# Cross-attention and mixture-of-experts block on one core: every product as plain 32-bit matmuls in two column halves, in place of three products of split operands

## The reference, cut to what matters

```
x = x + xattn(layernorm(x), ctx, w_q, w_k, w_v, w_o, b_o)
x = x + ffn(layernorm(x), router_w, router_b, w1, b1, w2, b2)
```

## Time and profile before

| | |
|---|---|
| median of three runs | 1013.3 us (1012.0 to 1015.47) |
| the profiled execution | 1018.17 us, its span 1016.3 us |
| TensorE busy | 979.9 us, 96% of the span |
| VectorE, ScalarE, GpSimd busy | 769.2, 624.3, 284.2 us |
| granted TensorE clock, mean | 0.993 |

### The profile page before, as it was taken

One profiled execution on the slowest core, in us unless ns is written; L12 is line 12 of the kernel. 1 busy time (PEld: TensorE's weight loads), 2 busy tenths in 40 slices (PEclk: granted clock), 3 DMA queues, 4 the chain that ended last, 5 costly groups with the idle time before them and its releaser, 6 DMA issues.

```text
span 1016.3 us, 23196 instructions
## 1 busy us (share of the span) xinstructions
PE 979.9 (96%) x8382; PEld 883.9 (87%) x8382; DVE 769.2 (76%) x2088; ACT 624.3 (61%) x1736; POOL 284.2 (28%) x440
## 2 busy tenths in 40 slices
PE   7889999999999999999999999999888999999996
PEld 6778888888888888888888888888678999999996
DVE  6897768878787888878787887878755666776662
ACT  5777767777776777777676777777514333344330
POOL 5542021314223131313223131311442333222233
PEclk9999999999999999999999999999999999999998
DMA  8440101101010101101010110001105543444522
GB/s 241 144 114 2 33 2 33 43 13 55 14 40 15 33 13 33 44 2 43 12 32 6 33 35 6 17 5 50 58 18 178 137 96 80 113 128 129 136 26 26
DMA packets 48431, 56.74 MB, mean 56 GB/s; under 512 B 5324, under 2 KB 44218, under 8 KB 48192
## 3 DMA queue, kind: packets, MB, share of 16 engines
q1 hardware_dynamic: 39488, 46.30, 14.7%
q0 software_dynamic: 8832, 8.98, 5.5%
HBM read 36.01 MB, written 24.20 MB: 59 GB/s over the span
## 4 chain that ended last, share of the span: by engine, by line
PE 71%; DVE 18%; ACT 5%; issue 4%; DMA 0%; POOLq 0%; POOL 0%; another core or an unknown queue 0%; ACTq 0%
PE psum L561 29%; PE psum L756 11%; PE psum L658 8%; PE psum L644 7%; PE psum L628 7%; PE psum L672 7%; DVE prob L985 5%; ACT prob L819 3%; DVE negmax L974 3%; DVE kl L922 1%; DVE al L922 1%; PE psum L566 1%; DVE stats L929 1%; PE psum L719 1%; DVE ql L963 1%
## 5 line engine op out<-in xcount | busy, mean ns | idle before, releaser
L819 ACT ACTIVATE prob<-psum,negmax 128x256 f32<-128x256 f32 x512 | 239.1, 484 | 81.6 <-DVE negmax L974 81.6
L771 ACT ACTIVATE probt<-psum 128x512 f32<-128x512 f32 x256 | 157.6, 617 | 53.4 <-PE psum L644 51.1
L974 DVE TENSOR_REDUCE negmax<-psum 128x2 f32<-128x512 f32 x256 | 160.0, 683 | 22.0 <-PE psum L628 21.9
L985 DVE TENSOR_SCALAR prob<-prob,invtot 128x256 f32<-128x256 f32 x512 | 168.0, 392 | 4.5
L644 PE MATMUL psum<-ident,prob 128*128 128x128 f32 x1024 | 154.4, 275 | 3.3 <-DVE prob L985 1.7
L644 PEld LDWEIGHTS psum<-ident,prob 128*128 128x128 f32 x1024 | 120.5, 142 | 14.5 <-issue 4.4
L898 ACT ACTIVATE hid<-psum,b1t 128x640 f32<-128x640 f32 x64 | 50.9, 795 | 133.2 <-PE psum L561 133.2
L658 PE MATMUL psum<-probt,v 128*64 128x256 f32 x1024 | 124.6, 385 | 0.8 <-ACT probt L771 0.8
L541 POOL DMA_INDIRECT out_rows<-y,rowi x40 | 65.7, 1644 | 174.5 <-DVE y L1137 169.6
L505 POOL DMA_INDIRECT slot_table<-row,picki x64 | 64.7, 1011 | 170.2 <-DVE picki L1087 143.2
L819 ACT ACTIVATION_READ_ACCUMULATOR prob<-psum,negmax 128x1 f32 x512 | 111.2, 217 | 0.0
(11 more groups left out here) (159 smaller groups left out, 2738.4 us busy)
## 6 DMA issues: line engine op xcount, KB each, us to landing
w1r<-in_w SPq DMA_DIRECT2D x8, 1024.0 KB, 8.1
w2r<-in_w SPq DMA_DIRECT2D x8, 1024.0 KB, 10.4
slot_table<-blank SPq DMA_DIRECT2D x8, 662.5 KB, 9.8
rows<-slot_table SPq DMA_DIRECT2D x7, 662.5 KB, 5.4
xin<-in_x SPq DMA_DIRECT2D x16, 256.0 KB, 3.0
out_rows<-x SPq DMA_DIRECT2D x16, 256.0 KB, 3.2
c<-in_ctxt SPq DMA_DIRECT2D x16, 128.0 KB, 3.1
c<-in_ctxt SPq DMA_DIRECT2D x32, 64.0 KB, 2.9
```

The costliest lines, as they stand in the source:

```text
L771: copy = lambda dst, src, **kw: act.activation(dst, src, ACT.Copy, **kw)
L819: last = act.activation(prob[:, m % 2, u, qb, :], psum[:, u, qb * S:(qb + 1) * S], ACT.Exp, bias=negmax[:, m % 2, u, qb:qb + 1], accum_out ...
L974: dve.tensor_reduce(negmax[:, m % 2, u, :], psum[:, u, :].rearrange("p (q s) -> p q s", q=ST), AX.X, ALU.max, negate=True).then_inc(sem("m ...
L985: last = dve.tensor_scalar(prob[:, m % 2, u, qb, :], prob[:, m % 2, u, qb, :], invtot[:, m % 2, u, qb:qb + 1], None, ALU.mult)
```

## The change

All splits go. Every operand is kept once in plain 32 bits, and every product is issued in two halves of 64 stationary columns, whose outputs lie in the two halves of the PSUM partitions. `scores` are issued as four 64-row by 64-column tiles for each query block. Turnings become products with the unit matrix, also in two halves. `warm` issues plain 32-bit products over the whole width. Weights are loaded once and stay in place; w1 and w2 of an expert go straight to one of two buffers, the first two during the attention. The 64 unused rows of `wk_s`, `c1` and `wv_s` are zeroed once by VectorE. The copies from PSUM that are left: ScalarE does `xt`, `q`, `v`, the turned probabilities and `x2t`; VectorE does `k`, `pv` and the turned rows. GpSimd loses the context split and the weight splits. The rows ring has three buffers (`RRING`), the context ring three (`CRING`). `hid` keeps all 8 blocks of an expert. `k(0)` is moved ahead of `xt(0)`.

```diff
-    xt, q, k = "xt xt_hi xt_lo", "q q_hi q_lo", "k k_hi k_lo"
-    pv = "pv a_hi a_lo"
+    xt, q, k, pv = "xt xt_sb", "q q_sb", "k k_sb", "pv a_sb"
+    out = [*steps("ln1_stats ln1_root ln1", 0), ("warm", 28), *steps(k, 0), ("warm", 8), *steps(xt, 0),
+           *steps(q, 0), *steps("scores max0 max1 exp0", 0), *steps(q, 1), *steps("max2 max3", 0), *steps(k, 1),
...
             def products(dst, terms):
+
                 for j, (lhs, rhs) in enumerate(terms):
-                    mm = pe.matmul(dst, lhs, rhs, start=(j == 0), stop=(j == len(terms) - 1))
+                    for h in range(2):
+                        hs = slice(h * HD, (h + 1) * HD)
+                        mm = pe.matmul(dst[hs, :], lhs[:, hs], rhs, start=(j == 0), stop=(j == len(terms) - 1))
                 return mm
+
+            def turned(dst, src):
+                return products(dst, [(src, ident[:, :])])
 
             def warm(at):
                 for j in range(at):
-                    pe.transpose(psum[:, 4, j % 4 * P:(j % 4 + 1) * P], ident[:, :], ident[:, :])
+                    pe.matmul(psum[:, 4, j % 4 * P:(j % 4 + 1) * P], ident[:, :], ident[:, :], start=True, stop=True)
...
                     mm = products(dst[:, cc * S:(cc + 1) * S],
-                                  [(w[:, k, cols], a[:, b % 2, k, :]) for k in range(DC)
-                                   for w, a in ((wqh, xth), (wqh, xtl), (wql, xth))])
+                                  [(wq_s[:, k, cols], xts[:, b % 2, k, :]) for k in range(DC)])
...
-                products(dst, [(c0h[:, b % 2, tt], wvh[:, 0, cols]), (c0l[:, b % 2, tt], wvh[:, 0, cols]),
-                               (c0h[:, b % 2, tt], wvl[:, 0, cols]), (c1s[:, b % 2, tt], wvh[:, 1, cols]),
-                               (c1s[:, b % 2, tt], wvl[:, 1, cols])]).then_inc(sem("v"), 1)
+                products(dst, [(c0[:, b % CRING, tt], wv_s[:, 0, cols]),
+                               (c1[:, b % CRING, tt], wv_s[:, 1, cols])]).then_inc(sem("v"), 1)
...
                     for qb in range(ST):
-                        cols = slice(qb * P, (qb + 1) * P)
-                        for j, (a, w) in enumerate(terms):
+                        for half in range(2):
                             for h in range(2):
-                                r = slice(h * HD, (h + 1) * HD)
-                                mm = pe.matmul(psum[:, 2 * cc + h, qb * S:(qb + 1) * S], a[r, m % 2, cc, cols],
-                                               w[r, m % 2, cc, :], start=(j == 0), stop=(j == len(terms) - 1))
+                                r, part = slice(h * HD, (h + 1) * HD), slice(half * HD, (half + 1) * HD)
+                                cols = slice(qb * P + half * HD, qb * P + (half + 1) * HD)
+                                mm = pe.matmul(psum[part, 2 * cc + h, qb * S:(qb + 1) * S], qs[r, m % 2, cc, cols],
+                                               ks[r, m % 2, cc, :], start=True, stop=True)
...
-                        mm = pe.transpose(psum[:, TURN_BANK[u], kb * S + qb * P:kb * S + (qb + 1) * P],
-                                          prob[:, m % 2, u, qb, kb * P:(kb + 1) * P], ident[:, :])
+                        mm = turned(psum[:, TURN_BANK[u], kb * S + qb * P:kb * S + (qb + 1) * P],
+                                    prob[:, m % 2, u, qb, kb * P:(kb + 1) * P])
...
-                    for j, (a, w) in enumerate(((ah, woh), (ah, wol), (al, woh))):
-                        mm = pe.matmul(dst[:, 0:D], a[:, b % 2, c, tt], w[:, c, :], start=(c == 0 and j == 0),
-                                       stop=(c == PAIRS - 1 and j == 2))
+                    for h in range(2):
+                        hs = slice(h * HD, (h + 1) * HD)
+                        mm = pe.matmul(dst[hs, 0:D], a[:, b % 2, c, tt][:, hs], wo_s[:, c, :], start=(c == 0),
+                                       stop=(c == PAIRS - 1))
...
                         mm = products(psum[:, 2 * (at % 2) + half, 0:HALF],
-                                      [(w[:, kk, cols], a[:, r, kk, hs]) for kk in range(DC)
-                                       for w, a in ((w1h[r], bufh), (w1h[r], bufl), (w1l[r], bufh))])
+                                      [(w1_s[:, r, kk, cols], buf[:, r, kk, hs]) for kk in range(DC)])
...
                         if s == 0:
-                            pe.wait_ge(sem("hid_lo"), HC * e + j + 1)
-                        for m, (a, w) in enumerate(((hidh, w2h[r]), (hidh, w2l[r]), (hidl, w2h[r]))):
-                            mm = pe.matmul(dst, a[:, j, ss], w[:, j, :], start=(j == 0 and m == 0),
-                                           stop=(j == HC - 1 and m == 2))
+                            pe.wait_ge(sem("gelu"), HC * e + j + 1)
+                        for h in range(2):
+                            hs = slice(h * HD, (h + 1) * HD)
+                            mm = pe.matmul(dst[hs, :], hid[:, j, s * P + h * HD:s * P + (h + 1) * HD],
+                                           w2_s[:, r, j, :], start=(j == 0), stop=(j == HC - 1))
...
+                if b in (4, 6):
+                    load_w((b - 4) // 2)
...
             def k(n):
-                dve.wait_ge(sem("k_hi"), n + 1)
-                rest_of(kl[:, n % 2, :, :], work_bank("k", n).rearrange("p (c s) -> p c s", c=2),
-                        kh[:, n % 2, :, :]).then_inc(sem("k_lo"), 1)
+                dve.wait_ge(sem("k"), n + 1)
+                if n >= 2:
+                    dve.wait_ge(sem("scores"), 4 * (n - 1))
+                dve.tensor_copy(ks[:, n % 2, :, :], work_bank("k", n).rearrange("p (c s) -> p c s", c=2))\
+                   .then_inc(sem("k_sb"), 1)
```

More of the change, by code:

```diff
@@ L138, in timeline @@
-            *steps("ln2_stats ln2_root", e), ("scatter", c), *steps("x2t x2t_sb logits", d), ("warm", 14),
+            *steps("turn0 copy0", m), *steps("turn1 copy1", m), *steps(half[1], m), *steps("pick scatter", c),
+            ("o", ST * d + 1), ("x2add", ST * d + 1), *steps("ln2_stats ln2_root", d), *steps(pv, m - 1),
+            *steps("turn2 copy2", m), *steps("turn3 copy3", m), *steps(pv, m), *steps("o x2add", ST * e),
+            *steps("o x2add", ST * e + 1), ("ln2", d), *steps("ln2_stats ln2_root", e),
@@ L139, in timeline @@
+            *steps("x2t x2t_sb logits", d), ("warm", 14),
             *steps("bias shift gate_exp gate", d), ("ln2", e), ("rank", d), *steps("x2t x2t_sb", e),
             *steps("pos slot keys", d), ("logits", e), ("warm", 18), *steps("bias shift gate_exp", e),
-            *steps("pick scatter", d), *steps("gate rank pos slot keys pick scatter", e),
-            ("w_lo", 2), ("w_lo", 3), ("warm", 90)]
+            *steps("pick scatter", d), *steps("gate rank pos slot keys pick scatter", e), ("warm", 90)]
@@ new lines, in build @@
+        c1 = sb(es, "c1", [CRING, S])
+        v = sb(es, "v", [2, ST, INNER])
+        a = sb(es, "a", [2, PAIRS, S])
+        x2 = sb(es, "x2", [2, ST, D])
+        row = sb(es, "row", [3, ST, ROW])
+        x2t = sb(es, "x2t", [DC, S])
+        bo_all = sb(es, "bo_all", [D])
+        rwt = sb(es, "rwt", [DC, NE])
+        rb_all = sb(es, "rb_all", [NE])
+        upto = sb(es, "upto", [P], BF16)
+        ones = sb(es, "ones", [P], BF16)
+        lower = sb(es, "lower", [NE, NE])
+        slot0i = sb(es, "slot0i", [NE], I32)
@@ L204, in build @@
+        chosen = sb(es, "chosen", [ST, NE], BF16)
+        before = sb(es, "before", [NE], BF16)
+        pick, same = (sb(es, n, [2, ST]) for n in ("pick", "same"))
+        picki = sb(es, "picki", [3, 2, ST], I32)
         early = ExitStack()
[L205 to L208, removed]
+        prob = sb(early, "prob", [2, UNITS, ST, S])
+        qs = sb(early, "qs", [2, 2, S])
@@ L209, in build @@
+        probt = sb(early, "probt", [2, UNITS, ST, S])
+        ks = sb(early, "ks", [2, 2, S])
         early.close()
[L210 to L218, removed]
@@ L237, in build @@
[L237 to L251, removed]
@@ L264, in build @@
[L264 to L272, removed]
-        def pieces(at):
-            return piece(*SPLITS[at], raw[at])
@@ L940, in ln_apply @@
                 last.then_inc(sem(which), 1)
-            def split(w):
-                dve.wait_ge(sem("split_hi"), w + 1)
-                whole, head, rest_ = pieces(w)
-                rest_of(rest_, whole, head).then_inc(sem("split_lo"), 1)
             def ln1_stats(b):
```

469 lines of the change are left out of this document (156 added, 313 removed).

## The result

The changed kernel takes 1298.85 us (median of four runs, 1298.51 to 1299.15) against 1014.33 us of the kernel before in the same comparison: a ratio of 1.2809, 95% interval 1.2782 to 1.2835. It is slower by 28%. The forecast was 1315 us with a range of 1285 to 1430.

The account below looks back on a forecast made before the run. TensorE, busy 96% of the span, was taken as the bound: 1016.3 + 238 (attention) + 57 (experts) + 10 (warm-up) - 3 (start and rise) = 1318 us of span, forecast about 1315 us, range 1285 to 1430.

Parts of the forecast that it names:

- The main step: In TensorE's products, 128 by 128 with 256 columns takes two pairs of 0.216 us: 0.432 us against 0.36 before.
- Turnings: Each 128 by 128 turning on TensorE goes from 0.11 to 0.216 us; the probabilities' 64 add 6.8 us a batch.
- the rivals: A turning's pairs held by loads (0.27 us each, 1385 us total, chance 0.11) or halves not overlapping (0.432, 1580 us, 0.04).
- factor of four: Skill's rule for turnings: losing the transpose mode makes each 0.44 us, some 1580 us in all; chance 0.04.
- Scores: Sixteen 64 by 64 tiles a period in the attention, four overlapping: 1.93 us against 1.62, +1.2 us a batch.
- rival 1: The four tiles of scores overlap only in twos: +1.73 us a period, +111 us, 1425 us in all; chance 0.12.
- unchanged, 0: The attention's pv already has the new form, so its cost in a batch changes by 0 us.
- The changes of tiling that fall away: Hand-overs saved because most steps now have one tiling: up to -15 or -20 us, within the likeliest case's range.
- `logits` and `pos` keep their form: In the attention's batch sum, these two steps were taken as unaltered and given no added cost.
- start, rise and warm-up together: Opening of the kernel and change-over to the experts: start and rise -3 us, the 90 warm-up products +10.
- The warm-up: The 90 products before the experts hold up the first rows' turning by 90 x 0.11 = 10 us.
- VectorE's and ScalarE's relief: Dropped copies and splits bring 0 in steady state, 5 us either side; TensorE's 6.7 us standstill in the rise counts against start costs.

Follow-up runs that it names:

- Run 7: The kernel before, with a fourth term (remainder by remainder) added to every split product: 1215.16 us against 1019.15, ratio 1.1919.
- run 2: The changed kernel, with products and turnings issued over the whole 128 columns (pv and scores keep their tiles): 1320.77 us, ratio 1.3034.
- run 8: The kernel before, with its 1232 turnings as plain products with the unit matrix over the whole width: 1159.99 us against 1019.15, ratio 1.1379.
- run 1: The changed kernel, with all 1232 turnings again done by one pe.transpose over the whole width: 1231.67 us, ratio 1.2143.
- run 3: The changed kernel, with scores in two row halves over all 128 columns, 8 matmuls a period instead of 16 tiles: 1300.32 us, ratio 1.2821.
- run 4: The changed kernel, with 45 in place of 90 warm-up products between attention and experts: 1290.40 us, ratio 1.2719.
- Run 5: The changed kernel, with VectorE doing its copies of k and pv and its row maxima twice: 1360.66 us, ratio 1.3360.

## Why the prediction was right

**The main step held.** It was that a product in halves costs two pairs of 0.216 us, read from `pv`. In the trace after, `q` and `k` with 16 instructions and `v` with 8 of double length take 1.71 to 1.73 us, eight such pairs (or four of double length). An expert came to 36.68 us for 36.7, `down` to 17.27 for 17.3. Run 7 shows from the other side that TensorE's passes are paid one by one, and run 2 that it is the passes and not the halves: a wide plain product takes the same 0.43. The four passes are worked out and not seen: a plain product is two instructions, and each takes the time of twice its columns.

**Turnings** were the largest term, and the size came out in part by luck. 0.216 us each was taken, with 0.27 and 0.432 as the rivals; four take 0.87 to 0.88 us, 0.22 each, and run 8 finds 141 us for them alone. But the 0.44 us of a unit before counted something twice: ahead of `k`, `v` and `o` the next product started after 0.36, and the rest stood at that product's head, which its own price held too. Without waits the turnings went from 111 to 231 us, +120 where 109 were forecast. Some 10 us of waits that vanished from that row brought the difference back to 110. The Trainium skill's factor of four for the transpose mode (TensorE: Matmul & The Clock Gate, Terms) is not what this kernel sees: 121.7 us of turnings became 231.7, a factor of 1.9, and 242.3 in run 8, a factor of 2.0. Its other statement, that column tiling excludes the mode (TensorEngine Tiling, Restrictions), no run here tests: in run 1 the transposes ran over the whole width.

**Scores:** four tiles overlap. 1.88 us a period where 1.93 was forecast, and rival 1 (3.66) is out by the trace after and by run 3.

**The excess.** The sum gave 1318 us of span where 1296.9 were measured, 21 too many; the forecast of 1315 us had 5 of them taken off again, which leaves 16. By the table, terms set too high come to some 28 us and terms set too low to 7. `pv` was costed "unchanged, 0" and got 8 us cheaper, `q` came out 5 us cheaper than the sum had it. Run 2 returns both: with wide products around it `pv` is back at 120.2 us and `q` at 118.0. The changes of tiling that fall away had been put into the range and not into the sum; they belong in the sum. The sentence "`logits` and `pos` keep their form" was wrong about `logits`, which goes through `products()`: 6 us. In `scores` (3 us) the hand-over was 0.16 us and not 0.2, in `o` (2 us) a step before took 2.96 and not 2.88, and the 3 us of `v` are the waits that its row held before. Too low were start, rise and warm-up together, 7 us against the 11 of the warm-up row (the waits that vanished in the rise stand in other rows), and all turnings with `k` by 3 us.

**The warm-up** was put at 10 us for the 90 products. In the traces the 90 went from 12.4 us, waits included, to 20.3, so 8 us more; run 4 takes 45 out and gets 8.5 back, until the rows' arrival is what TensorE waits for.

**VectorE's and ScalarE's relief** was put at 0 in the steady part and at some 7 us in the rise. Nearly so: of the 36.4 us in which TensorE stood still 17.0 are left. That the lighter engines did this and not the slower TensorE is made likely by runs 7 and 8, which take 196 and 141 us more on TensorE beside an unrelieved VectorE and in which it still stands still for 36.3 and 38.9 us. In the attention up to the change-over 11 us of waits went, 8 of them up to the third batch; 7 more went in the change-over, where the longer warm-up now stands. No run puts all of the work back. Run 5 marks the limit of the argument: work ahead of VectorE's reads of the router's banks costs 56 us with the engine at 62%.

## What to carry to other kernels

When an engine is busy all the time, count its passes before anything else: here three passes of split operands against four of plain ones decided, and the copies that the split needs were nearly free, as their engines were early. Price a new form by the nearest step that already has it, and count the changes of tiling between neighbours as a term of the sum. A small step of the bound engine may also be the cover of another engine's copy, so move it only after looking at what stands behind it.

## What the runs showed of the hardware

A plain 32-bit product costs the same over the whole width and in two column halves (1.73 us for four products with 256 columns, either way). Halves gain where the columns are too few to set the pace: the router's product with 8 columns went from 13.4 to 7.3 us in all. That the loads set its pace is the likely reason; no run separates them from another fixed cost of an instruction. Four 64 by 64 tiles run at once (1.88 us a period, against 1.93 in two row halves). A change of tiling between neighbouring steps costs 0.13 to 0.2 us here (run 1: 0.13 to 0.15; run 2, between `pv` and `q`: 0.2).
